# GpSimd takes the last three operations of the rotated query and key splits, and the order of work is planned anew, in a four-layer transformer kernel

## What is computed

```python
q, k, v = (t[:, :, 0], t[:, :, 1], t[:, :, 2])
return (_apply_rope(q, cos, sin), _apply_rope(k, cos, sin), v)   # t * cos + rot * sin
...
s = jnp.einsum('bqhd,bkhd->bhqk', q, k) * scale
s = jnp.where(mask, s, jnp.finfo(s.dtype).min)
a = jax.nn.softmax(s, axis=-1)
return jnp.einsum('bhqk,bkhd->bqhd', a, v)
```

## Time and profile before

| | |
|---|---|
| median of 3 runs | 2919.24 us (2916.59 to 2923.46) |
| the profiled execution, its own time | 2916.84 us |
| its span, first to last instruction | 2915.0 us |
| mean granted clock of PE | 0.976 of full speed |
| busy: PE, DVE, ACT, POOL | 2728.5, 1893.7, 1425.8, 590.3 us |
| instructions | 47,676 |

### The profile page before, as it was taken

The page is one execution under the profiler, slowest core; times in us unless marked ns, Lnnn a source line. Parts: engine busy times, 40 slices in busy tenths (PEclk is TensorE's granted clock), DMA queues, the critical chain, the costliest instruction groups (busy, mean ns, idle before and its releaser), DMA issues. The chain is left out here.

```text
span 2915.0 us, 47676 instructions
## 1 busy us (share of the span) xinstructions
PE 2728.5 (94%) x15136; PEld 1351.8 (46%) x15136; DVE 1893.7 (65%) x4209; ACT 1425.8 (49%) x2579; POOL 590.3 (20%) x999
## 2 busy tenths in 40 slices
PE   8999999999989999999988888898999999999899
PEld 5444344335544424334455566656645323224456
DVE  5977388642574783866344889668974884885621
ACT  3455635574445583566644444333221674785441
POOL 2110001131331110331125323411020010112510
PEclk9999999999999999999998999999999999999899
DMA  6333122433452312233066516521420322123621
GB/s 207 69 104 107 41 72 71 112 89 98 144 172 53 114 51 67 91 115 95 22 186 186 167 50 195 146 85 60 147 60 1 116 60 52 45 61 108 183 92 38
DMA packets 268153, 286.78 MB, mean 98 GB/s; under 512 B 70665, under 2 KB 207243, under 8 KB 267275
## 3 DMA queue, kind: packets, MB, share of 16 engines
q1 hardware_dynamic: 256651, 282.28, 33.0%
q0 software_dynamic: 11264, 1.46, 0.3%
HBM read 167.43 MB, written 114.72 MB: 97 GB/s over the span
## 5 line engine op out<-in xcount | busy, mean ns | idle before, releaser
L1570 ACT ACTIVATE probs<-ring_b 128x512 f32<-128x512 f32 (+1 forms) x1728 | 921.8, 599 | 457.9 <-PE ring_b L1429 359.9
L1748 DVE TENSOR_REDUCE row_max<-ring_a 128x1 f32<-128x1024 f32 x512 | 602.0, 1218 | 151.7 <-PE ring_a L1385 150.9
L1429 PE MATMUL ring_b<-q_ring,k_ring 100*128 100x512 bf16 x1536 | 526.8, 381 | 10.5 <-ACT probs L1570 2.8
L1385 PE MATMUL ring_a<-k_ring,q_ring 96*128 96x512 bf16 x1536 | 450.1, 383 | 27.9 <-DVE row_max L1748 16.1
L1462 PE MATMUL ring_c<-probs,v_and_ones 128*17 128x512 f32 x3072 | 402.0, 599 | 1.8 <-ACT probs L1570 1.2
L1745 DVE CUSTOM_DVE_ANT_0 w_mlp<-ring_a,w_mlp 128x1024 bf16<-128x1024 f32 x256 | 302.1, 1222 | 49.6 <-PE ring_a L1385 48.4
L1868 POOL CAST neg_max_parts<-neg_max 16x128 bf16<-16x128 f32 x112 | 37.6, 336 | 1392.1 <-ACT neg_max L1564 1141.3
L1429 PEld LDWEIGHTS ring_b<-q_ring,k_ring 100*128 100x128 bf16 x1536 | 145.7, 97 | 349.9 <-issue 241.5
L1385 PEld LDWEIGHTS ring_a<-k_ring,q_ring 96*128 96x128 bf16 x1536 | 135.5, 98 | 250.5 <-issue 153.6
L1485 PE MATMUL ring_b<-h_feat,w_mlp 128*128 128x512 f32 x512 | 230.3, 595 | 1.4 <-ACT h_feat L1541 0.8
L1497 PE MATMUL ring_a<-w_mlp 128*128 128x256 f32 x1024 | 226.1, 380 | 5.0 <-DVE w_mlp L1803 2.4
(11 more groups left out here) (143 smaller groups left out, 3346.4 us busy)
## 6 DMA issues: line engine op xcount, KB each, us to landing
q_ring<-scr_q SPq DMA_DIRECT2D x128, 384.0 KB, 4.3
scr_q<-split SPq DMA_DIRECT2D x64, 384.0 KB, 2.6
k_ring<-scr_k SPq DMA_DIRECT2D x64, 384.0 KB, 5.0
scr_q<-split SPq DMA_DIRECT2D x64, 256.0 KB, 3.0
scr_out<-out_stage SPq DMA_DIRECT2D x128, 128.0 KB, 2.5
scr_out<-out_stage SPq DMA_DIRECT2D x64, 256.0 KB, 2.4
h_feat<-scr_out SPq DMA_DIRECT2D x56, 256.0 KB
reciprocals<-scr_recip SPq DMA_DIRECT2D x56, 256.0 KB
```

The lines of the kernel that those rows point to most:

```text
L1385: last = mm(ps[:, half * BLOCK:(half + 1) * BLOCK], q[0:PARTS, h, t * P:(t + 1) * P], k_view(g)[0:PARTS, h, half * BLOCK:(half + 1) * BLOC ...
L1429: last = mm(ps[:, :], k_view(g)[0:ROWS, h, s.kt * P:(s.kt + 1) * P], q[0:ROWS, h, q0:q0 + BLOCK], start=not g.masked, stop=True)
L1570: f(PT[0:n, s.pt, :], ps[0:n, :], ACT.Exp, **kw).then_inc(b_evac, 1)
L1748: v.tensor_reduce(NM[:, s.nm, s.u:s.u + 1], ps, AX.X, ALU.max).then_inc(a_evac, 1)
```

## The change

It has two parts.

**Tails.** `TAILS = (0, 3)`. For the rotated splits of layers 0 and 3 of 512 columns, the step "split" becomes two. "rotate" keeps L1349 on PE and the first four DVE operations (to L1694), and signals the new semaphore `turned`. "tail" does what L1697, L1698 and L1699 did, on POOL, and signals `tail_done`; `raw` is given back only behind it, and the scratch write waits for it. These are 8 splits each in 0a, 0b, 3a and 3b for self-attention, and 4 each in 3a and 3b for cross-attention: 40 in all. The two rotated splits of context keys (154 columns) stay on DVE, as do all splits that are not rotated.

**Order.** All rank tables are other numbers, `REACH` allows POOL to wait 0.8 us and SP 0.3 us for a step of lower rank, and the layer norms of the second batch may begin at 320 instead of 100.

```diff
 RANK = dict(
-    init=(9.3, 10.7, 9.3, 11.3),
...
+    init=(17.7, 14.9, 14.9, 3.7),
...
-REACH = dict(PE=0.0, ACT=0.0, DVE=0.05, POOL=0.0, SP=0.2)
-DELAY = (7.5, 100)
...
+REACH = dict(PE=0.0, ACT=0.0, DVE=0.05, POOL=0.8, SP=0.3)
+DELAY = (7.5, 320)
...
+TAILS = (0, 3)
...
-        d = yield do("split", ([("PE", 0.264 if ck else 0.86)] if rope else []) + [("DVE", (2.08 if rope else 0.84) if ck else 4.3 if rope else 1.79)],
-                     after=[s], ring="a" if rope else None, counts=["split_n"], of=s, rope=rope, l=l)
+        if rope and l in TAILS and not ck:
+            t = yield do("rotate", [("PE", 0.86), ("DVE", 2.55)], after=[s], ring="a", counts=["turned_n"], of=s, l=l)
+            d = yield do("tail", [("POOL", 3.5)], after=[t], counts=["tail_n"], of=s, turned=t, l=l)
+        else:
+            d = yield do("split", ([("PE", 0.264 if ck else 0.86)] if rope else []) + [("DVE", (2.08 if rope else 0.84) if ck else 4.3 if rope else 1.79)],
+                         after=[s], ring="a" if rope else None, counts=["split_n"], of=s, rope=rope, l=l)
...
+                        if s.kind == "rotate":
+                            v.tensor_copy(parts[:, 0, :], r).then_inc(turned, 1)
...
+                elif s.kind == "tail":
+                    f = s.of
+                    r = RAW[:, f.raw, 0:f.width]
+                    parts = SPLIT[:, f.split, :, 0:f.width]
+                    pool.wait_ge(turned, s.turned.turned_n + 1)
+                    link(g_.tensor_tensor(out=r, in0=r, in1=parts[:, 0, :], op=ALU.subtract))
+                    link(g_.tensor_copy(parts[:, 1, :], r))
+                    g_.tensor_tensor(out=parts[:, 2, :], in0=r, in1=parts[:, 1, :], op=ALU.subtract).then_inc(tail_done, 1)
```

More of the change, by code:

```diff
@@ L283 @@
 RANK = dict(
-    init=(9.3, 10.7, 9.3, 11.3),
-    mod=(2.1, -3, 3.8, 5.8),
-    prep=(4.6, -12, -4, 4.6),
-    out=(-3, -12, -12, -12),
-    ctx=(3.1, 20, 5.1, 7.1),
-    load=(20, -1.2, 0.8, -3.2),
-    cross_f=(11.3, 6.1, 5.7, 3.1),
-    cross_s=(6.3, -1.1, -4.2, 1.0),
-    mlp=(9.0, 8.0, 4.0, -1.4),
-    self_f=(-12, 18.8, -12, 11.8),
-    self_pv=(15, 24, 7.1, 24),
-    self_s=(-9.8, 8.2, -5.8, 8.2),
-    tk=(10.1, 0.1, -12, 9.9),
-    tk_s=(-0.5, 6.1, -9.2, -5.2),
-    win_f=(-6, -12, -4, 0),
-    win_s=(10.5, 8.5, 7.5, 6.5),
-)
-REACH = dict(PE=0.0, ACT=0.0, DVE=0.05, POOL=0.0, SP=0.2)
-DELAY = (7.5, 100)
-SECOND = dict(init=-15, mod=-9, prep=-4, out=4, ctx=-24, load=-14, cross_f=7,
-              cross_s=13, mlp=-3, self_f=-3, self_pv=24, self_s=-8, tk=-5, tk_s=-20,
-              win_f=-19, win_s=4)
-LATER = (-7, -6.5, -5, -40)
+    init=(17.7, 14.9, 14.9, 3.7),
+    mod=(14.5, 1.8, 0.8, -7.2),
+    prep=(7.3, 1, -7.9, -5),
+    out=(-7, -10, -10, -10),
+    ctx=(4.1, 20.0, -3.0, 20.0),
+    load=(23, 3.8, 24, 16),
+    cross_f=(-6.0, 18.8, -4.7, -6.0),
+    cross_s=(2.4, 2.4, 18.2, 4.9),
+    mlp=(4.0, 2.0, 5.0, 5.7),
+    self_f=(-5, 23, -8, 6),
+    self_pv=(10.5, 24, 5.5, 24),
+    self_s=(-1, 2.1, -3.9, -11),
+    tk=(-4.9, 6.2, -12, -3.0),
+    tk_s=(-11, -10, -12, -3),
+    win_f=(-1.5, -7.9, -7.9, 13.9),
+    win_s=(7.2, 11.2, 9.5, 13.5),
+)
+REACH = dict(PE=0.0, ACT=0.0, DVE=0.05, POOL=0.8, SP=0.3)
+DELAY = (7.5, 320)
+SECOND = dict(init=0, mod=-22, prep=-7, out=-5, ctx=-12, load=-7, cross_f=24,
+              cross_s=8, mlp=19, self_f=5, self_pv=23, self_s=-2, tk=-7, tk_s=7,
+              win_f=-18, win_s=10)
+LATER = (-9, -8.5, -24, -40)
 FILL_ONE = 0.11
+TAILS = (0, 3)
 def rank_of(kind, l, b, blk):
@@ L996, in blocks_kernel, with split_ended @@
         xn_ready, ctxn_ready = sem("xn_ready"), sem("ctx_norm_ready")
-        split_done = sem("split_done")
+        split_done, turned, tail_done = sem("split_done"), sem("rotated"), sem("tail_done")
+        def split_ended(eng, d):
+            if d.kind == "tail":
+                eng.wait_ge(tail_done, d.tail_n + 1)
+            else:
+                eng.wait_ge(split_done, d.split_n + 1)
         scr_in = [sem(f"scratch_written_{i}") for i in range(SPLITS)]
@@ L1153, in _ @@
                         elif r.kind == "scratch":
-                            sp.wait_ge(split_done, r.done.split_n + 1)
+                            split_ended(sp, r.done)
                         elif r.kind == "ctx_put":
@@ L1163, in _ @@
                     d, s = s.done, s.of
-                    sp.wait_ge(split_done, d.split_n + 1)
+                    split_ended(sp, d)
                     for j, parts in SCRATCH[s.which[-1]]:
@@ L1344, in _ @@
                     last.then_inc(b_full, 1)
-                elif s.kind == "split" and s.rope:
+                elif s.kind == "rotate" or s.kind == "split" and s.rope:
                     f = s.of
@@ L1550, in _ @@
                         else:
-                            act.wait_ge(split_done, s.raw_last.split_n + 1)
+                            split_ended(act, s.raw_last)
                     col = {"q": 4 if s.cross else 0, "k": 2, "ck": 6}[s.which] + s.hh
@@ L1676, in _ @@
                     v.tensor_tensor(GB[:, 0, :], ps[:, 0:FEAT], ROWS_IN[:, s.row.slot, :], ALU.add).then_inc(a_evac, 1)
-                elif s.kind == "split":
+                elif s.kind in ("split", "rotate"):
                     f = s.of
@@ L1680, in _ @@
                     parts = SPLIT[:, f.split, :, 0:f.width]
-                    if s.rope:
+                    if s.kind == "rotate" or s.rope:
                         dve.wait_ge(tables_in, 16 * 3)
@@ L1693, in _ @@
                         link(v.tensor_tensor(r, r, rot[:, 0:f.width], ALU.add))
-                        link(v.tensor_copy(parts[:, 0, :], r))
+                        if s.kind == "rotate":
+                            v.tensor_copy(parts[:, 0, :], r).then_inc(turned, 1)
+                        else:
+                            link(v.tensor_copy(parts[:, 0, :], r))
                     else:
                         dve.wait_ge(b_evac, f.bn + 1)
-                    link(v.tensor_tensor(r, r, parts[:, 0, :], ALU.subtract))
-                    link(v.tensor_copy(parts[:, 1, :], r))
-                    v.tensor_tensor(parts[:, 2, :], r, parts[:, 1, :], ALU.subtract).then_inc(split_done, 1)
+                    if s.kind == "split":
+                        link(v.tensor_tensor(r, r, parts[:, 0, :], ALU.subtract))
+                        link(v.tensor_copy(parts[:, 1, :], r))
+                        v.tensor_tensor(parts[:, 2, :], r, parts[:, 1, :], ALU.subtract).then_inc(split_done, 1)
                 elif s.kind in ("v", "ctx_v"):
@@ L1722, in _ @@
                             else:
-                                dve.wait_ge(split_done, s.raw_last.split_n + 1)
+                                split_ended(dve, s.raw_last)
                     src = ps[0:n, 0:nt * FEAT].rearrange("p (t h d) -> p t h d", t=nt, h=HEADS)
```

## The result

The changed kernel takes 2937.36 us (median of 4 runs, 2935.95 to 2938.36), the kernel before 2917.91 us on the same chip. The ratio is 1.007, with a 95% interval of 1.0053 to 1.0088: **slower by 19.5 us**, where 12 us faster was forecast. The profiled execution took 2938.36 us, its span is 2936.6 us.

A forecast was written before the change was run, and what follows sets the result against it. PE bounds in name only; DVE, full in the top-16 stretch, is on the path that sets the end. Terms -14.3 + 2.9 + 3.6 - 6.0 + 1.8 = -12.0 us, from 2919.24 to 2907.2 us, range 2890 to 2928.

The forecast's parts named there:

- The tails off DVE: Batch b's top-16 work: eight 3a tails of 1.79 us each leave DVE, all on the path, 14.3 us less.
- collisions: Top-16 stretch: POOL's tails hold up DVE operations, half a hit of 0.72 us per tail, +2.9 us.
- The second rival: Top-16 stretch: every POOL operation of eight tails holds DVE up, 17.3 us instead of 2.9, total 2921.6; chance 0.16.
- A tail on POOL: Each moved tail takes 1.325 + 0.9 + 1.325 = 3.6 us on POOL (3.0 to 3.7), 1.8 longer than on DVE.
- The start: 0a's first splits: two chains per raw buffer each end 1.8 us later, +3.6 us, bounds 0 and 7.2.
- not 2 to 5: Sign of a right forecast at the start: first row maximum comes 2 to 5 us later than 72.
- the other 32 tails: Tails outside the top-16 work, 57 us of DVE: counted as nothing, PE being full or DVE mostly waiting there.
- The new order: First top-16 unit of batch a to layer 2's end: 166 fewer stand-ins, -6.0 us left for the order, bounds 0 and 17.4.
- The last cross-attention: Layer 3's cross-attention: first chain of queries ends 1.8 us later without cover, +1.8 us, bounds 0 and 28.8.
- third rival: Last cross-attention: POOL becomes the queue, each of eight tails holds back maxima, 28.8 instead of 1.8, total 2934.2; chance 0.20.
- a longer last stage: Named sign of POOL being the queue on the path, beside maxima waiting for `tail` in layer 3's cross-attention.

The follow-up runs named there:

- e9: Kernel before, its engine lists kept, only the 16 tails of 3a's and 3b's self-attention moved to POOL: ratio to before 0.9971, 8.5 us faster.
- e12: Kernel before, its lists kept, only the 8 tails of 0a moved to POOL: ratio to before 1.0009, 2.6 us.
- e14: Changed kernel, its lists kept, the 16 tails of 0a and 0b back on DVE: ratio to before 1.007.
- e10: Kernel before, its lists kept, only the 16 tails of 0a and 0b moved to POOL: ratio to before 1.0035, 10.2 us slower.
- e13: Kernel before, its lists kept, only the 8 tails of 0b moved to POOL: ratio to before 1.0016, 4.7 us.
- e8: Changed kernel, its lists kept, the 8 tails of layer 3's cross-attentions back on DVE: ratio to before 1.0059.
- e2: Kernel before, lists kept on PE, ACT and SP, all 40 tails moved to POOL: ratio to before 1.0013, 3.8 us slower.
- e4: Changed kernel's tables without tails, all splits whole on DVE, lists planned anew: 2937.7 us, ratio to before 1.0088.
- e7: Changed kernel, same lists, 2,183 stand-ins instead of 1,635: ratio to before 1.0069.

## Why the prediction was wrong

**The tails off DVE, -14.3 with +2.9 of collisions: right in kind, a third too high.** In e9 the stretch gained 7.6 us (155.7 to 148.1) and the kernel 8.5 (5.0 to 12.2 by the interval). Its hits were not what ate the rest: the rows of L1703, L1705 and L1707 in that stretch have means of 820, 692 and 426 ns, where the same work took 772, 692 and 426 before, 0.4 us for all eight. But in e9 DVE stood idle for 4.0 us before its rotations, for PE's rotation matmul (L1361), where before it never did. With DVE relieved another engine came last at times, so not all of the 14.3 us was on the path, as I had put it. In the changed kernel the rotations of that stretch, from 2000 to 2130 us, had means of 819, 800 and 741 ns for L1703, L1705 and L1707, 0.47 us more for each chain, 3.8 us for eight, beside my 2.9. **The second rival** is therefore real in kind and at most a quarter of its 17.3 us; that the stretch got shorter with less work on DVE shows that DVE was the bound.

**A tail on POOL, 3.6 us:** 3.1. The cast was 0.69 us for my 0.9 (0.61 in the median), and the two subtractions 2.43 for my 2.65. The cast lies between my price and the 0.45 us that I had worked out as an estimate from the Trainium skill (GPSIMD Engine Reference, 4.1 Engine selection). Its sum for a tail, 3.1 us, was met by luck: its cast was too short by as much as my subtractions, which it had taken over, were too long.

**The start, +3.6:** in e12's profile 0a's first row maximum came 2.8 us later and its first exponential 2.1: about right. The 2.6 us of e12 as a whole (-1.2 to 6.7) are no measure of it, since they hold the wait that ended at 183 us as well. In the changed kernel the first row maximum came at 79.24 us, 7.1 later and not 2 to 5; there the order had moved it too, since with the tails back on DVE (e14) it came at 80.4.

**"For the other 32 tails I count nothing: where those of 0b and 3b stand, PE is full."** This step failed for layer 0, for 0b and for 0a's last two tails, which stand beside 0a's attention as well. PE was full because everything arrived in time, the one load read above with an estimated 1.6 us to spare. What stands behind a tail on POOL and behind its scratch write on SP came late as well, and in e10 a wait of 1 us was followed by 1.7 us of missing clock. e13 measured 4.7 us (1.5 to 7.6) for 0b, e10 10.2 for both batches. In the old lists this eats all that the top-16 stretch gains. The other half of that step, that at the start and in the cross-attention of layer 3 DVE waits more than it works, was misread from the earlier trace rows: DVE worked 28.63 and 40.82 of 50 us at the start and 37.29 in the cross-attention. Nothing came of it, as e12 and e8 show no gain or loss there that can be told from nothing.

**The new order, -6.0, bounds 0 and -17.4: the step that decided, and its sign was wrong.** With the tails on POOL the new order costs 16.6 us (e2 against the changed kernel); without tails the new tables cost 25.6 (e4). I had priced the whole order by the plan's stand-ins in one stretch, 166 fewer in the top-16 work, and the order everywhere else at nothing. The stand-ins are counted from gaps that the plan assumes, not from gaps on the chip. The stretch lies in two stages, up to 2a's MLP (65 fewer) and up to 2b's cross-attention (95 fewer). Together they take 659.0 us in the changed kernel and 664.3 in e2. In the mean of the profiles it is 659 with the new lists and tails (changed, e7, e8, e14) and 663 with the old ones (e2, e9), so a gain near my 6.0 may well be there, though kernels with the same lists differ by more than that. The order's cost lies where the stand-ins hardly changed. In the same kind of means it is some 16 us in the last stage, where 5 were added behind that place, and some 8 over layers 0 and 1. What in layers 0 and 1 does it was not tried.

**The last cross-attention, +1.8:** e8 says 3.2 and e2's remainder 2.1, neither of which can be told from 0 or from 1.8. The **third rival** (+28.8, a total of 2934.2) comes nearest to the result by its number and by one sign that I had named for it, a longer last stage, but it is refuted: with its eight tails back on DVE the stage took 256.9 us instead of 254.7. Its sign fitted two mechanisms, and only the experiment told them apart. That an order as such could lose was no rival of mine at all, and my bound for it ended at 0; it should have been one, since the order was the larger part of the diff.

Terms put together: -8.5 (3 self) + 10.2 (layer 0) + 2.1 (cross) + 16.6 (order) = +20.4, and 19.5 was measured. This sum closes by construction and proves nothing: 2.1 was the rest of e2, and 16.6 the rest between e2 and the changed kernel. Independent of each other are only e9 and e10, whose sum of 1.7 agrees with e2's 3.8.

**The version that beats both** is e9: the kernel before, its order untouched, with the tails of layer 3's self-attention alone on POOL. 2907.13 us beside 2914.73 for the kernel before, measured together, 0.9971 (0.9958 to 0.9983), and 1% faster than the changed kernel.

## What to carry to other kernels

Move work to an idle engine only where the engine it leaves is full, and count what is queued in order behind it on the new engine and on the queue that waits for it: transfers that have nothing to do with it come late too. When a change brings a new static order, treat the order as a change of its own with a price on either side of zero; the plan's fillers say what the plan believed, not what the chip will do. Keep some long matmul work beside the last latency-bound piece, but not so much that this piece ends after it; here the shortest last stages had 12 of its 32 exponentials left when that work began.
